# Head scores from two fp32r parts in four row bands instead of three bf16 parts in two, with the expert weights loaded later

## The chip, the cores and the metric

The kernel runs on 1 core of a Trainium2 chip. The metric is the device time of one execution in microseconds (us). A core has TensorE (PE; its weight loads are shown as PEld), VectorE (DVE), ScalarE (ACT), GpSimd (POOL) and SyncE (SP, which here only issues DMAs), each with its own instruction stream; they meet at semaphores.

## The reference, cut to what matters

A layer of attention and a mixture of experts, in fp32, over 32 batches of 256 tokens with 128 features:

```python
qkv = x @ W_qkv.T + b_qkv            # 16 heads, head size 8
att = einsum('bthd,bshd->bhts', q, k) / sqrt(8)
att_v = einsum('bhts,bshd->bthd', softmax(att), v)
x = layernorm(x + att_v @ W_out.T + b_out)
# 8 experts of 128x128, two chosen per token, and a shared one
h = silu(routed @ w1[e].T) * (routed @ w3[e].T);  out = h @ w2[e].T
x = layernorm(x + moe(x))
```

The routing picks the two best experts of each token, so x must be exact enough that no choice flips. This is why scores are built from several parts of lower precision and not from one.

## The kernel before, in words

**Two stages.** The first is attention over 32 batches, the second the experts over 16 groups of 512 tokens. The stages share SBUF: buffers of the second (`places`) lie on `q_stack` and `k_stack`.

**The scores.** The product of q and k over a head has a contraction of only 8. q and k are each split into three bf16 parts on POOL (L428 to L455: casts, differences, remainders `rk`, `rq`), and six pairs of parts (`QPART`, `KPART`) are stacked, so that one matmul with 48 rows gives the exact score. The parts go by DMA to DRAM (L336, L341) and come back stacked (L304): `q_stack` and `k_stack` hold 128 partitions in two halves of 64, even heads in one and odd heads in the other. The scores are computed twice. `row_maxima_scores` (L651) has queries on the output partitions, and DVE reduces 512 columns to negative row maxima (L937). The maxima, as two bf16 parts (POOL L406, L408), are transposed (L784), copied to `max_rows` by DVE (L978) and put by two DMAs (L310) in two more rows of `q_stack`. `shifted_scores` (L638, 50 rows) has keys on the output partitions and includes the maxima; ACT takes the exponential (L515). `values` (L666) multiplies by v in fp32, four heads at a time in column strips of 32. Each of the two kinds of scores has three PSUM banks, used in turn.

**The slots.** The attention is software-pipelined over slots s = -4 to 34. In slot s: SP loads x of batch s+5, q and k of batch s+4 are projected (`t.proj`: L735, L752), batch s+3 is stacked and its v projected (`t.stack`: L748), s+2 has its row maxima (`t.maxi`), s+1 has them transposed and stacked (`t.neg`), s has its exponentials (`t.soft`), s-1 is normalised and transposed (`t.tail`: L768, L806, DVE L971, L987), s-2 goes through output projection and layer norm (`t.norm`: L728, L949 to L959, POOL L435, L444, L800), s-3 through the gate (`t.gated`: L775). Each engine has a fixed order written out in its `slot` function. On TensorE it is eight pairs of heads, p = 0 to 7: 4 shifted-score matmuls and 4 maxima matmuls in turn, then one block of other work: output and K projection after p = 0, values after p = 1, 3, 5 and 7, V and Q projection after p = 2, transposes, gate and maxima after p = 4, transposes back after p = 6. DVE does a reduction per head, with the sum of the residual after head 1, its statistics after 2 and 4, and reciprocal, `max_rows`, `logits` and `att_tok` after head 9.

**The start.** DVE clears `k_stack` and `v_aug` for all four ring places. ACT makes kf and qf of batch 0 and then issues all constants (`load_constants`, L499 and L503): small ones, `w1T`, `w3T`, `w2T` (576 KB each) and 16 DMAs for the v bias. Near slot 0, ACT rounds w1 and w3 to fp32r (L584), and POOL makes the remainders (L461).

**The experts.** 16 groups, each 9 experts: `up` is 2 x 3 fp32r matmuls (L673 to L675), `down` one fp32 matmul (L829), with DVE (L1001, L1011), ACT (L603, L616) and POOL (L476) between; L835 closes the group before.

## Time and profile before

| | us |
|---|---|
| median of 3 runs | 806.11 (803.26 to 808.59) |
| the profiled execution | 806.83 |
| its span, first to last instruction | 804.8 |
| PE busy | 757.6 (94%) |
| DVE busy | 639.9 (80%) |
| ACT busy | 521.4 (65%) |
| POOL busy | 480.6 (60%) |

Busy time is the union of an engine's recorded instructions. Records of one engine can overlap (a matmul's record is longer than the distance to the next), so that an engine whose work is paced by another can still look full. The profile's slices show the two stages: in the first DVE is at nine tenths or more in most slices, in the second at six or seven; PE is at nine tenths in both after the first slices.

### The profile page before, as it was taken

What the parts mean: (1) busy time and instruction counts of PE and PEld (TensorE: products, weight loads), DVE (VectorE), ACT (ScalarE), POOL (GpSimd) and SP (SyncE); (2) the same over time, 40 slices, a digit from 0 to 9 for tenths busy, and PEclk for the clock granted to TensorE, in tenths of its full rate; (3) what the DMA queues carried; (4) which work ended last, traced back from release to release, by engine and by line L of the source; (5) the groups of instructions that cost most, each with busy time, mean ns of one, the idle gap of its engine ahead of it and who ended that gap; (6) DMA issues with size and microseconds to landing.
All of it is one profiled execution on the core that took longest, in us unless ns stands there. A gap on an engine that the chain in (4) does not pass through costs nothing.

```text
span 804.8 us, 18923 instructions
## 1 busy us (share of the span) xinstructions
PE 757.6 (94%) x6148; PEld 460.7 (57%) x6148; DVE 639.9 (80%) x1382; ACT 521.4 (65%) x1047; POOL 480.6 (60%) x653
## 2 busy tenths in 40 slices
PE   1699999999999999999998699999999999999996
PEld 0234555555555555555554466666666666666663
DVE  5578999999999999999997286666666666666765
ACT  1138888888888888888888265555555555555542
POOL 3446767667667677676633345555666565656654
PEclk9999999999999999999999789999999999999998
DMA  5653656656565566566520442455644444444541
GB/s 162 166 128 114 175 160 169 170 157 155 165 165 158 169 169 161 160 166 164 149 76 22 131 116 75 131 132 131 130 129 123 118 126 116 128 119 117 133 120 52
DMA packets 201534, 108.79 MB, mean 135 GB/s; under 512 B 10480, under 2 KB 201072, under 8 KB 201456
## 3 DMA queue, kind: packets, MB, share of 16 engines
q1 hardware_dynamic: 200048, 105.88, 49.5%
q10 hardware_dynamic: 1408, 1.91, 0.9%
q8 instruction: 44, 0.72, 0.4%
q14 instruction: 34, 0.28, 0.1%
HBM read 73.41 MB, written 33.82 MB: 133 GB/s over the span
## 4 chain that ended last, share of the span: by engine, by line
PE 87%; issue 3%; DVE 3%; POOL 3%; DMA 2%; ACT 1%; SPq 1%; POOLq 0%; DVEq 0%; ACTq 0%
PE bank L666 15%; PE bank L829 14%; PE bank L638 10%; PE bank L673 8%; PE bank L675 8%; PE bank L674 8%; PE bank L651 7%; PE bank L748 3%; PE bank L728 2%; PE bank L768 2%; PE bank L735 2%; PE bank L752 2%; PE bank L800 2%; PE bank L775 1%; DVE negmax L937 1%
## 5 line engine op out<-in xcount | busy, mean ns | idle before, releaser
L937 DVE TENSOR_REDUCE negmax<-bank 128x2 f32<-128x512 f32 x512 | 320.1, 679 | 25.3 <-PE bank L651 22.7
L515 ACT ACTIVATE probs<-bank 128x512 f32<-128x512 f32 x512 | 291.7, 605 | 61.0 <-PE bank L638 57.2
L651 PE MATMUL bank<-k_stack,q_stack 48*128 48x256 bf16 x1024 | 163.7, 283 | 9.4 <-DMA k_stack<-k_parts_dram 5.3
L673 PE MATMUL bank<-x_hi,hi_w 128*128 128x512 f32 x288 | 166.5, 578 | 1.3 <-DVE q_stack L1011 0.9
L616 ACT ACTIVATE q_stack<-k_stack 128x512 f32<-128x512 f32 x128 | 80.7, 631 | 122.7 <-DVE k_stack L1001 121.2
L638 PE MATMUL bank<-q_stack,k_stack 50*128 50x256 bf16 x1024 | 156.8, 275 | 2.9 <-ACT probs L515 2.5
L1001 DVE TENSOR_TENSOR k_stack<-bank,probs 128x512 f32<-128x512 f32 x128 | 88.2, 689 | 75.5 <-PE bank L675 69.6
L666 PE MATMUL bank<-probs,v_aug 128*32 128x256 f32 x2048 | 137.9, 387 | 0.4 <-ACT attT L526 0.4
L638 PEld LDWEIGHTS bank<-q_stack,k_stack 50*128 50x128 bf16 x1024 | 75.4, 95 | 86.7 <-ACT probs L515 44.5
L675 PE MATMUL bank<-x_lo,hi_w 128*128 128x512 f32 x288 | 115.3, 400 | 0.0
L674 PE MATMUL bank<-x_hi,lo_w 128*128 128x512 f32 x288 | 115.3, 400 | 0.0
L603 ACT ACTIVATE probs<-probs 128x512 f32<-128x512 f32 x128 | 79.3, 620 | 22.7 <-DMA probs<-route_dram 22.0
L476 POOL TENSOR_TENSOR k_stack<-k_stack,probs 128x512 f32<-128x512 f32 x48 | 61.9, 1290 | 52.8 <-DVE k_stack L1011 47.6
L651 PEld LDWEIGHTS bank<-k_stack,q_stack 48*128 48x128 bf16 x1024 | 71.8, 96 | 27.7 <-DVE negmax L937 11.7
L666 PEld LDWEIGHTS bank<-probs,v_aug 128*32 128x32 f32 x2048 | 53.8, 109 | 49.7 <-issue 15.0
L829 PE MATMUL bank<-k_stack,w_sb 128*128 128x512 f32 x160 | 81.5, 592 | 0.0
L673 PEld LDWEIGHTS bank<-x_hi,hi_w 128*128 128x128 f32 x288 | 55.2, 192 | 39.7 <-issue 28.8
L476 POOL TENSOR_TENSOR k_stack<-q_stack,probs 128x512 f32<-128x512 f32 x32 | 41.1, 1283 | 60.1 <-DVE q_stack L1011 51.2
L476 POOL TENSOR_TENSOR place<-k_stack,probs 128x512 f32<-128x512 f32 x48 | 62.1, 1294 | 24.4 <-PE bank L829 23.5
L674 PEld LDWEIGHTS bank<-x_hi,lo_w 128*128 128x128 f32 x288 | 55.6, 193 | 36.1 <-issue 29.1
L1011 DVE TENSOR_TENSOR k_stack<-bank,q_stack 128x512 f32<-128x512 f32 x96 | 65.5, 682 | 4.3 <-POOL k_stack L476 3.6
L675 PEld LDWEIGHTS bank<-x_lo,hi_w 128*128 128x128 f32 x288 | 55.1, 191 | 13.5
(101 smaller groups left out, 1061.4 us busy)
## 6 DMA issues: line engine op xcount, KB each, us to landing
probs<-route_dram SPq DMA_DIRECT2D x128, 256.0 KB, 5.9
q_stack<-q_parts_dram SPq DMA_DIRECT2D x64, 192.0 KB, 3.3
k_stack<-k_parts_dram SPq DMA_DIRECT2D x64, 192.0 KB, 4.1
k_parts_dram<-k_parts SPq DMA_DIRECT2D x32, 192.0 KB, 2.1
q_parts_dram<-q_parts SPq DMA_DIRECT2D x32, 192.0 KB, 2.1
xT_sb<-xT SPq DMA_DIRECT2D x32, 128.0 KB, 2.2
k_parts_dram<-k_parts SPq DMA_DIRECT2D x32, 128.0 KB, 2.0
q_parts_dram<-q_parts SPq DMA_DIRECT2D x32, 128.0 KB, 2.0
```

Of the source, the lines that this page charges most:

```text
L476: pool.tensor_tensor(hid_s[n % DEPTH], hid[n % DEPTH], weight2_b[n - 1], ALU.mult).then_inc(hids_set, 1)
L515: nc.scalar.activation(probs[h][:], score_ps[EXP_BANK[h]][:].rearrange("p (j t) -> p j t", j=NT), ACT.Exp).then_inc(exp_done, 1)
L616: nc.scalar.activation(act[n % DEPTH], gated[n % DEPTH] if n else up1_ps[0][:], ACT.Silu).then_inc(act_set, 1)
L638: mm = pe.matmul(score_ps[EXP_BANK[h]][:, j * T:(j + 1) * T], k_stack[b.ring][first:last, h // 2, j * P:(j + 1) * P], q_stack[b.ring][firs ...
L651: mm = pe.matmul(max_ps[MAX_BANK[h]][:, i * T:(i + 1) * T], q_stack[b.ring][first:last, h // 2, i * P:(i + 1) * P], k_stack[b.ring][first: ...
L666: mm = pe.matmul(av_ps[32 * hh:32 * hh + 32, half * T:(half + 1) * T], v_aug[b.ring][:, 2 * j + half, u, hh, :], probs[4 * quad + hh][:, j ...
L673: pe.matmul(ps[:], w_hi[m][:, n, :], hi[:], start=start, stop=False)
L674: pe.matmul(ps[:], w_lo[m][:, n, :], hi[:], start=False, stop=False)
L675: return pe.matmul(ps[:], w_hi[m][:, n, :], lo[:], start=False, stop=stop)
L829: pe.matmul(down_ps[r][:], w2_sb[:, n, :], (hid_s if n else hid)[n % DEPTH], start=(n == 0), stop=(n == NE - 1)).then_inc(down_mm, 1)
L937: nc.vector.tensor_reduce(negmax[b.ring % 2][:, :, column], max_ps[MAX_BANK[h]][:].rearrange("p (i s) -> p i s", i=NT), AX_X, ALU.max, neg ...
L1001: nc.vector.tensor_tensor(gated[n % DEPTH], up1_ps[n % DEPTH][:], weight_b[e], ALU.mult).then_inc(gated_set, 1)
```

## The change: what it does

- q and k are split into two fp32r parts instead of three bf16 parts; three pairs of parts make 24 rows a head (26 with the maxima) instead of 48 (50). POOL issues 4 split operations a batch instead of 8.
- The stacks hold four bands of 32 partitions, one head of four in each, as 4-byte elements: `[128, 4 heads, 256]` instead of `[128, 8, 256]` in bf16, the same bytes. The score matmuls are fp32r. Shifted scores use band h % 4, maxima take head h ^ 2, so that the four matmuls of one step of a pair lie in four different bands. The loops over n (which half of the 256) and h change places, so that both heads of a pair are worked on together.
- SP issues 2 DMAs each for the parts of k and q (3 before), 8 for the stacks (4 before), 4 for the maxima (2 before). `max_rows` is fp32, 8 of its partitions to a DMA.
- For batch 0, q is projected into `av_ps` without waiting for kf, and split by DVE between the clearing of ring places 1 and 2. ACT waits for the clearing of the place that it writes, not for all four.
- The small constants are issued at the end of the slot that projects batch 1; w1, w3 and w2 one by one in slots 2, 3 and 4; their split is done in six pieces in slots 4 to 9. The v bias takes 2 DMAs to DRAM and one back instead of 16.
- In the expert stage, `places` lie elsewhere, the load of `x1_sb` is issued after the weights of the group, and a group's result is written one group later in SP's order.

```diff
-PARTS = 3
-QPART = (0, 0, 0, 1, 1, 2)
-KPART = (0, 1, 2, 0, 1, 0)
-TWO_ONES = float(np.array([0x3F803F80], np.uint32).view(np.float32)[0])
+PARTS = 2
+QPART = (0, 0, 1)
+KPART = (0, 1, 0)
 HALF = 64
+FOUR, BAND = 4, 32
...
+        q_stack = [sb(f"q_stack{r}", [P, QUADS, T]) for r in range(RING)]
+        k_stack = [sb(f"k_stack{r}", [P, QUADS, T]) for r in range(RING)]
...
+        qf, kf = (sb(n, [P, T]) for n in ("qf", "kf"))
+        q_parts, k_parts = ([sb(f"{n}{r}", [P, PARTS, T], F32R) for r in range(2)] for n in ("q_parts", "k_parts"))
+        max_two = [sb(f"max_two{r}", [P, NT, FOUR, 2, QUADS], BF16) for r in range(2)]
+        max_rows = sb("max_rows", [2 * H, T])
...
+        def steps(b, more):
+            return more if b.c == 0 else b.count(4, more - 2)
+        def expert_slot(m):
+            return 2 + m
+        def split_slot(m, n):
+            return 4 + m * (NE // 3) + n // 3
+        def q_place(b):
+            return av_ps[:, 0:T] if b.c == 0 else right
...
-                        for u in range(2):
-                            sp.dma_start(stack[b.ring][HALF * u:HALF * u + ROWS, :, :],
-                                         dram[b.ring].rearrange("(g u) d c t -> u (d c) g t", u=2)[u]).then_inc(stack_in[b.ring], 16)
+                        for u in range(FOUR):
+                            sp.dma_start(stack[b.ring][BAND * u:BAND * u + ROWS, :, :],
+                                         dram[b.ring].rearrange("(g u) d c t -> u (d c) g t", u=FOUR)[u]).then_inc(stack_in[b.ring], 16)
                 b = t.neg
                 if b.live:
                     sp.wait_ge(max_rows_set, b.count(1, 1))
-                    for u in range(2):
-                        sp.dma_start(q_stack[b.ring][HALF * u + ROWS:HALF * u + ROWS + 2, :, :],
-                                     max_rows[H * u:H * u + H, :]).then_inc(max_in[b.ring], 16)
+                    for u in range(FOUR):
+                        sp.dma_start(q_stack[b.ring][BAND * u + ROWS:BAND * u + ROWS + 2, :, :],
+                                     max_rows[2 * QUADS * u:2 * QUADS * (u + 1), :]).then_inc(max_in[b.ring], 16)
...
-                    sp.wait_ge(split_step, b.count(8, 4))
-                    for part in range(PARTS):
-                        first, count = QPART.index(part), QPART.count(part)
-                        assert KPART[first:first + count] == tuple(range(count))
-                        sp.dma_start(k_parts_dram[b.ring, :, :, first:first + count].rearrange("h d c t -> (h d) c t"),
-                                     k_parts[b.ring % 2][:, 0:count, :]).then_inc(parts_out, 16)
-                    sp.wait_ge(split_step, b.count(8, 8))
-                    for part in range(PARTS):
-                        first, count = QPART.index(part), QPART.count(part)
-                        sp.dma_start(q_parts_dram[b.ring, :, :, first:first + count].rearrange("h d c t -> (h d) c t"),
-                                     q_parts[b.ring % 2][:, part:part + 1, :].to_broadcast([P, count, T])).then_inc(parts_out, 16)
+                    sp.wait_ge(split_step, steps(b, 2))
+                    k_place, k_from = k_parts_dram[b.ring].rearrange("h d c t -> (h d) c t"), k_parts[b.ring % 2][:].bitcast(F32)
+                    sp.dma_start(k_place[:, 0:2], k_from).then_inc(parts_out, 16)
+                    sp.dma_start(k_place[:, 2:3], k_from[:, 0:1]).then_inc(parts_out, 16)
+                    if b.c == 0:
+                        sp.wait_ge(q_split_set, 2)
+                    else:
+                        sp.wait_ge(split_step, steps(b, 4))
+                    q_place, q_from = q_parts_dram[b.ring].rearrange("h d c t -> (h d) c t"), q_parts[b.ring % 2][:].bitcast(F32)
+                    sp.dma_start(q_place[:, 0:2], q_from[:, 0:1].to_broadcast([P, 2, T])).then_inc(parts_out, 16)
+                    sp.dma_start(q_place[:, 2:3], q_from[:, 1:2]).then_inc(parts_out, 16)
...
-                    if e == 4:
+                    if e == E - 1:
                         if past(g, 2):
                             sp.wait_ge(res2_set, g - 1)
                         sp.dma_start(x1_sb[r][:], x1_dram[bass.ds(g * GT, GT), :, :].rearrange("i p c -> p i c")).then_inc(x1_in[r], 16)
-                    if e == 3 and past(g, 2):
-                        write_out(g - 1)
+                    if e == 3 and past(g, 3):
+                        write_out(g - 2)
                 if isinstance(g, int) and g == 1:
                     route_to_dram(slice(CHUNKS - 1, CHUNKS), 2)
                     sp.wait_ge(route_out[1], 16)
 
             groups(sp, group)
+            write_out(GROUPS - 2)
...
-                    pool.wait_ge(split_step, p.count(8, 1))
-                    pool.tensor_tensor(rk[:], kf[:], k_split[:, 0, :], ALU.subtract).then_inc(split_step, 1)
...
+                if p.live and p.c:
                     pool.wait_ge(qk_f, p.count(2, 2))
-                    pool.tensor_tensor(k_split[:, 2, :], rk[:], k_split[:, 1, :], ALU.subtract).then_inc(split_step, 1)
                     pool.tensor_copy(q_split[:, 0, :], qf[:]).then_inc(split_step, 1)
-                    pool.wait_ge(split_step, p.count(8, 5))
-                    pool.tensor_tensor(rq[:], qf[:], q_split[:, 0, :], ALU.subtract).then_inc(split_step, 1)
+                    pool.wait_ge(split_step, steps(p, 3))
                     pool.tensor_tensor(q_split[:, 1, :], qf[:], q_split[:, 0, :], ALU.subtract).then_inc(split_step, 1)
-                    pool.wait_ge(split_step, p.count(8, 7))
-                    pool.tensor_tensor(q_split[:, 2, :], rq[:], q_split[:, 1, :], ALU.subtract).then_inc(split_step, 1)
-                    if p.c == RING and not p.looped:
-                        for m in range(2):
-                            pool.wait_ge(w_hi_set, m + 1)
-                            pool.tensor_tensor(w_lo[m][:], w_stage[m], w_hi[m][:], ALU.subtract).then_inc(w_lo_set, 1)
+                for m in range(2):
+                    for n in range(0, NE, 3):
+                        if t.soft.c == split_slot(m, n):
+                            pool.wait_ge(w_hi_set, m * (NE // 3) + n // 3 + 1)
+                            pool.tensor_tensor(w_lo[m][:, n:n + 3, :], w_stage[m][:, n:n + 3, :], w_hi[m][:, n:n + 3, :],
+                                               ALU.subtract).then_inc(w_lo_set, 1)
...
-                                 (gate_sb, gateT), (ebias_sb, ebias.to_broadcast([P, E])), (rank_sb, rank.to_broadcast([P, E])),
-                                 (w_stage[0], w1T), (w_stage[1], w3T), (w2_sb, w2T)):
+                                 (gate_sb, gateT), (ebias_sb, ebias.to_broadcast([P, E])), (rank_sb, rank.to_broadcast([P, E]))):
                     act_e.dma_start(dst[:], src).then_inc(c_in, 16)
-                for head in range(H):
-                    half, u, hh = head // 8, head // 4 % 2, head % 4
-                    row = half * 64 + hh * 2 * D + u * D
-                    act_e.dma_start(bv_sb[row:row + D, :], bv[0, 0:1, head * D:head * D + D].rearrange("o d -> d o")).then_inc(bv_in, 16)
+                for half in range(2):
+                    act_e.dma_start(bv_dram[HALF * half:HALF * half + HALF].rearrange("(g u d) o -> g u (d o)", g=4, u=2),
+                                    bv[0, 0:1, HALF * half:HALF * half + HALF].rearrange("o (u g d) -> (o g) u d", u=2, g=4)).then_inc(bv_out, 16)
+            def load_expert(m):
+                dst, src = ((w_stage[0], w1T), (w_stage[1], w3T), (w2_sb, w2T))[m]
+                act_e.dma_start(dst[:], src).then_inc(expert_in[m], 16)
...
-                            load_constants()
-                    if b.live and h == 12 and b.c == RING and not b.looped:
-                        act_e.wait_ge(c_in, 16 * 8)
+                        if b.c == 1:
+                            act_e.wait_ge(q_split_set, 2)
+                        elif b.later(1):
+                            act_e.wait_ge(split_step, steps(Batch(b.i, b.c - 1, B), 4))
+                        nc.scalar.activation(qf[:], q_place(b), ACT.Identity, bias=bqs[:, 0:1], scale=SCALE).then_inc(qk_f, 1)
+                    if b.live and h == 12:
                         for m in range(2):
-                            nc.scalar.activation(w_hi[m][:], w_stage[m], ACT.Copy).then_inc(w_hi_set, 1)
+                            for n in range(0, NE, 3):
+                                if t.soft.c == split_slot(m, n):
+                                    act_e.wait_ge(expert_in[m], 16)
+                                    nc.scalar.activation(w_hi[m][:, n:n + 3, :], w_stage[m][:, n:n + 3, :], ACT.Copy).then_inc(w_hi_set, 1)
+                        for m in range(3):
+                            if t.soft.c == expert_slot(m):
+                                load_expert(m)
+                if t.proj.c == 1:
+                    load_constants()
+                if t.proj.c == 2:
+                    act_e.wait_ge(bv_out, 16 * 2)
+                    act_e.dma_start(bv_sb[:], bv_dram).then_inc(bv_in, 16)
...
-                    pe.wait_ge(max_in[b.ring], b.lap(32, 32))
-                    if b.c == 0 and not b.looped:
-                        pe.wait_ge(c_in, 16 * 8)
+                    pe.wait_ge(max_in[b.ring], b.lap(64, 64))
                 if j == 0 and (b.later(1) or h >= EXP_BACK[h]):
                     pe.wait_ge(exp_done, b.count(H, h + 1 - EXP_BACK[h]))
-                first, last = HALF * (h % 2), HALF * (h % 2) + ROWS + 2
-                mm = pe.matmul(score_ps[EXP_BANK[h]][:, j * T:(j + 1) * T], k_stack[b.ring][first:last, h // 2, j * P:(j + 1) * P],
-                               q_stack[b.ring][first:last, h // 2, :], start=True, stop=True)
+                first, last = BAND * (h % FOUR), BAND * (h % FOUR) + ROWS + 2
+                mm = pe.matmul(score_ps[EXP_BANK[h]][:, j * T:(j + 1) * T],
+                               k_stack[b.ring][first:last, h // FOUR, j * P:(j + 1) * P].bitcast(F32R),
+                               q_stack[b.ring][first:last, h // FOUR, :].bitcast(F32R), start=True, stop=True)
                 if j == NT - 1:
                     mm.then_inc(score_mm, 1)
 
             def row_maxima_scores(b, h, i):
 
                 if i == 0 and h == 0:
-                    pe.wait_ge(stack_in[b.ring], b.lap(64, 64))
+                    pe.wait_ge(stack_in[b.ring], b.lap(128, 128))
                 if i == 0 and (b.later(1) or h >= MAX_BACK[h]):
                     pe.wait_ge(max_red, b.count(H, h + 1 - MAX_BACK[h]))
-                other = 1 - h % 2
-                first, last = HALF * other, HALF * other + ROWS
-                mm = pe.matmul(max_ps[MAX_BANK[h]][:, i * T:(i + 1) * T], q_stack[b.ring][first:last, h // 2, i * P:(i + 1) * P],
-                               k_stack[b.ring][first:last, h // 2, :], start=True, stop=True)
+                m = h ^ 2
+                first, last = BAND * (m % FOUR), BAND * (m % FOUR) + ROWS
+                mm = pe.matmul(max_ps[MAX_BANK[h]][:, i * T:(i + 1) * T],
+                               q_stack[b.ring][first:last, m // FOUR, i * P:(i + 1) * P].bitcast(F32R),
+                               k_stack[b.ring][first:last, m // FOUR, :].bitcast(F32R), start=True, stop=True)
...
-                    for h in (2 * p, 2 * p + 1):
-                        for n in range(NT):
+                    for n in range(NT):
+                        for h in (2 * p, 2 * p + 1):
...
+                        if t.proj.live and t.proj.c:
...
+                        pe.matmul(q_place(b), wq_sb[:], xT_sb[b.ring][:], start=True, stop=True).then_inc(q_mm, 1)
...
-            for r in range(RING):
-                flat = k_stack[r][:].rearrange("p h t -> p (h t)").bitcast(F32)
-                for u in range(2):
-                    dve.memset(flat[HALF * u + 32:HALF * u + HALF, :], TWO_ONES).then_inc(k_ones, 1)
+            def clear(r):
+                dve.memset(k_stack[r][:], 1.0).then_inc(k_ones, 1)
                 dve.memset(v_aug[r][:], 0.0).then_inc(v_clear, 1)
                 dve.wait_ge(v_clear, 2 * r + 1)
                 for u in range(2):
                     ins = dve.memset(v_aug[r][:, :, u, :, 2 * D + u:2 * D + u + 1], 1.0)
                 ins.then_inc(v_clear, 1)
+            clear(0)
+            clear(1)
+            q_split = q_parts[0]
+            dve.wait_ge(qk_f, 2)
+            nc.vector.tensor_copy(q_split[:, 0, :], qf[:]).then_inc(q_split_set, 1)
+            dve.wait_ge(q_split_set, 1)
+            nc.vector.tensor_tensor(q_split[:, 1, :], qf[:], q_split[:, 0, :], ALU.subtract).then_inc(q_split_set, 1)
+            clear(2)
+            clear(3)
...
-                        column = PAIRS * (1 - h % 2) + h // 2
+                        m = h ^ 2
+                        column = QUADS * (m % FOUR) + m // FOUR
```

## Rows read from the trace of the kernel before

**Rows 1.** By stretch: length; busy of PE, PEld, DVE, ACT, POOL; clock, DMA share, GB/s:
```profile
202.17:214.65 12.48, 12.48 (x156) 7.11 (x154) 12.19 (x27) 10.57 (x24) 8.56 (x16) 1.00 0.61 161
...
393.30:405.20 11.90, 11.66 (x151) 6.68 (x151) 11.64 (x27) 9.89 (x22) 7.46 (x14) 1.00 0.45 120
...
500.00:520.00 20.00, 20.00 (x76) 13.53 (x74) 13.17 (x26) 10.35 (x19) 12.55 (x10) 1.00 0.47 125
```

**Rows 2.** Timeline of TensorE: K projection of two slots, 24 slots apart:
```profile
92.03 0.60 PE L735 MATMUL bank<-xT_sb,wk_sb 128*128 128x256 f32 x2
...
387.41 0.38 PE L735 MATMUL bank<-xT_sb,wk_sb 128*128 128x256 f32 x1
```

**Rows 3.** Timeline of TensorE: the transposes of two neighbouring slots without projections:
```profile
405.15 0.44 PE L768 MATMUL bank<-used_first,attT 128*128 128x128 f32 x2
...
417.10 0.55 PE L768 MATMUL bank<-used_first,attT 128*128 128x128 f32 x3
```

**Rows 4.** Timeline of TensorE: one pair's scores and the values behind it:
```profile
203.25 0.28 PE L638 MATMUL bank<-q_stack,k_stack 50*128 50x256 bf16 x1
...
203.60 0.27 PE L638 MATMUL bank<-q_stack,k_stack 50*128 50x256 bf16 x1
203.79 1.07 PE L666 MATMUL bank<-probs,v_aug 128*32 128x256 f32 x16
```

**Rows 5.** Timeline of the weight loads, the same pair and the V projection:
```profile
203.25 0.09 PEld L638 LDWEIGHTS bank<-q_stack,k_stack 50*128 50x128 bf16 x1 [0.33 <-ACT probs L515]
203.25 0.09 PEld L651 LDWEIGHTS bank<-k_stack,q_stack 48*128 48x128 bf16 x1
...
203.79 0.59 PEld L666 LDWEIGHTS bank<-probs,v_aug 128*32 128x32 f32 x16 [0.21 <-issue]
...
205.34 0.52 PEld L748 LDWEIGHTS bank<-wv_sb,xT_sb 128*128 128x128 f32 x4 [0.21 <-issue]
```

**Rows 6.** Timeline of VectorE in one slot:
```profile
203.36 0.42 DVE L949 TENSOR_TENSOR res<-bank,x_bo 128x256 f32<-128x256 f32 x1
...
206.28 0.43 DVE L959 TENSOR_SCALAR var_eps<-mv 128x2 f32<-128x2 f32 x1
206.63 3.08 DVE L937 TENSOR_REDUCE negmax<-bank 128x2 f32<-128x512 f32 x5
209.86 0.36 DVE L971 RECIPROCAL recip_sum<-bank 128x32 f32<-128x32 f32 x1
...
210.86 4.40 DVE L937 TENSOR_REDUCE negmax<-bank 128x2 f32<-128x512 f32 x7
```

**Rows 7.** The line L959 alone, in the two slots without projections:
```profile
L959 DVE TENSOR_SCALAR var_eps<-mv x2: 169/169/169, 403.2 to 415.1; 128x2 f32<-128x2 f32 x2
```

**Rows 8.** Timelines of DVE, SP and PE: from the maxima's copy to the next slot:
```profile
222.62 0.21 DVE L978 COPY max_rows<-bank 32x256 bf16<-32x256 bf16 x1
...
222.86 1.26 SPq L310 DMA_DIRECT2D q_stack<-max_rows  x2
...
226.41 0.28 PE L638 MATMUL bank<-q_stack,k_stack 50*128 50x256 bf16 x1
```

**Rows 9.** The chain of waits at the start (start, us, what):
```profile
13.18 8.54 DMA q_parts_dram<-q_parts
...
23.12 4.29 DMA k_stack<-k_parts_dram
...
27.55 0.61 PE bank L651 x4
...
48.70 0.82 SPq L310
49.57 1.89 DMA q_stack<-max_rows
```

**Rows 10.** Timeline of ACT near slot 0:
```profile
64.41 2.21 ACT L584 ACTIVATE hi_w<-x1T 128x1152 fp32r<-128x1152 f32 x2
```

More of the change, by code:

```diff
@@ L133, in attention_moe_layer @@
         w_in, xT_in, x_in = sem("w_in"), [sem(f"xT_in{r}") for r in range(RING)], [sem(f"x_in{r}") for r in range(RING)]
-        c_in = sem("c_in")
+        c_in, bv_out, expert_in = sem("c_in"), sem("bv_out"), [sem(f"expert_in{m}") for m in range(3)]
+        q_split_set = sem("q_split_set")
         k_ones, v_clear, consts_set = sem("k_ones"), sem("v_clear"), sem("consts_set")
@@ L196, in attention_moe_layer @@
         LAG, HID_LAG = 4, 1
-        places = [stack[:].rearrange("p h t -> p (h t)").bitcast(F32)[:, n * G:(n + 1) * G]
-                  for stack in q_stack[:2] + k_stack[:2] + q_stack[2:] + k_stack[2:] for n in range(PAIRS * T // 2 // G)]
-        places += [sb(f"place{n}", [P, G])[:] for n in range(8)]
+        places = [parts[:].rearrange("p c t -> p (c t)").bitcast(F32) for parts in q_parts + k_parts]
+        places += [sb(f"place{n}", [P, G])[:] for n in range(10)]
+        places += [v[:].rearrange("p a u g c -> p (a u g c)")[:, n * G:(n + 1) * G] for v in v_aug for n in range(2)]
+        places += [attT[:].rearrange("p a t -> p (a t)")]
+        assert PARTS * T == G
         def take(count):
@@ L551, in slot @@
                             act_e.wait_ge(av_mm, b.count(4, 4 * (1 - RING)))
-                        elif not b.later(1):
-                            act_e.wait_ge(v_clear, 2 * RING)
+                        else:
+                            act_e.wait_ge(v_clear, 2 * (b.c + 1))
                         for u in range(2):
@@ L751, in slot @@
                     if b.live and p == PE_VQ:
-                        pe.matmul(right, wq_sb[:], xT_sb[b.ring][:], start=True, stop=True).then_inc(q_mm, 1)
+                        pe.matmul(q_place(b), wq_sb[:], xT_sb[b.ring][:], start=True, stop=True).then_inc(q_mm, 1)
                     if p == PE_TOK:
```

51 lines of the change are left out of this document (22 added, 29 removed).

## The prediction

> **What bounds the kernel now.** I read the busy time by stretch first. A slot of attention takes 12.3 to 12.5 us; in the one shown TensorE is busy for all of its 12.48 us and DVE for 12.19 [rows 1]. The distance of two K projections, 24 slots apart, gives the pitch: (387.41 - 92.03) / 24 = 12.31 us [rows 2]. In the expert stage TensorE is busy for 20.00 of 20.00 us, and DVE for only 13.17 [rows 1]. So TensorE sets the pace of both stages, but in attention DVE stands just behind it. How close, the two slots without projections tell: there TensorE has less to do and idles, and the pitch falls only to 417.10 - 405.15 = 11.95 us [rows 3]. That is DVE's own pace. I check it with DVE's timeline [rows 6]. Five reductions whose record is 0.68 us each span 3.08, so one follows another after (3.08 - 0.68) / 4 = 0.60 us, and 16 take 9.6. From the residual's sum at 203.36 to the reductions at 206.63 there are 3.27 us with three reductions in them, so 1.47 for sum, statistics and variance; reciprocal to `att_tok` take 210.86 - 209.86 = 1.00. The sum is 12.07 us. The slots without projections have a shorter L959: 0.17 us [rows 7] instead of 0.43 [rows 6]; in them POOL has no splitting to do.
>
> **The score matmuls.** A pair of heads takes 203.79 - 203.25 = 0.54 us before the next block starts [rows 4]: the last matmul starts 0.35 after the first, and 0.19 more go by until the next block. Eight matmuls go in pairs, one in each half of the array, four steps of 0.115. The change makes it two steps of four. Against it stands the weight load: bf16 loads have records of 0.09 us, the four fp32 loads of 128 columns span 0.52 with a mean of 0.19, so they follow each other after (0.52 - 0.19) / 3 = 0.11 us [rows 5]. No row shows an fp32r load in a band of 32 rows. I take 0.11, from that row. If the loads of four bands run side by side, a pair costs 0.11 for the first loads, 0.11 for one step and 0.19 until the next block: 0.41, 0.13 less, times 8 pairs = 1.05 us a slot, and TensorE needs 12.3 - 1.05 = 11.25. They do run side by side as far as rows show: the loads of the two halves both start at 203.25, and 16 fp32 loads in four strips of columns take 0.59 us together with records of 0.11 [rows 5]. The bounds are 0.30 a pair (nothing for the loads: 2 x 0.115 less than now, minus 0.01) and 1.07 (eight loads of 0.11 in turn, then 0.19).
>
> The Trainium skill (TensorE: Matmul & The Clock Gate, "Weight-path perf modes") says that the fast weight load is on only for 128 weights and types other than FP32. The records of 0.09 against 0.19 us agree. It speaks against this change, which takes the fast load away from 64 loads a slot. TensorEngine Tiling (Array Packing) of the same skill, "Key Properties", says that different tiles can load weights and multiply in parallel; by that the loss is paid once per pair, otherwise four times per step. No row shows four bands.
>
> **What a slot becomes.** With TensorE at 11.25, DVE is the bound. POOL issues four subtractions of 256 columns fewer, among them the one beside L959; this gives DVE up to 0.26 back: 12.07 - 0.26 = 11.8. Two things work against it. First, a pair now needs both its banks free before its first matmul, so TensorE can be less far ahead: pairs followed by values take 0.41 + 1.0 = 1.41 us on TensorE against 1.20 for two reductions, and DVE's surplus of work at the start of a slot and at the transposes makes up for all but some 0.16. That gives 11.96. Second, the maxima need four DMAs instead of two. SP issues two in 1.26 us, so 0.63 each; the copy ends at 222.83 and the next slot's scores start at 226.41, 3.58 later [rows 8]. At the start of the kernel, second issue to landing took 1.89 [rows 9], so landing is now some 2.5 after the copy and becomes 2.5 + 1.26 = 3.76 at 0.63 an issue, 3.4 at 0.45. DVE at its own pace wants the scores 3.5 after the copy. I take 0.1 to 0.15 for it: 12.1 us a slot. Gain: 0.2 x 24 = 4.8 us; with POOL's gift not given and the DMAs at 0.63, 12.3 or more and nothing or a loss; with neither drag 11.8 and 12. SP's other issues: stacks 4 more, parts 2 fewer; SP has some 7.4 us of issues in 12.3 now, and the stack issues end about 2 us before the maxima, so those 4 x 0.47 = 1.9 are just hidden; without that cover they delay the maxima's DMAs one for one. The two slots before the layer norms run (68 to 92) were paced by TensorE and gain about 0.4 each: 0.8. Exponentials on ACT (10.57 of 12.48 busy) stay hidden. The drain at the end of attention gains 0.3.
>
> **The start.** On the chain, the parts of q of batch 0 take 8.54 us to land after 13.18, while 1.7 MB of constants are on the way; the stack follows with 4.29 from 23.12, and the first maxima start at 27.55 [rows 9]. After the change: kf at 6.7 as now, two POOL operations (0.4 + 0.7), k's DMAs at 7.9. q's projection no longer waits for kf, ACT finishes qf near 7.5, DVE has cleared two places by 6 and splits q by 8.2. SP issues four DMAs by 9.9; without the constants they land after about 2.1 (as the maxima's 1.89): 11.7. Then 8 stack DMAs instead of 4: 8 x 0.47 = 3.8, the last lands 3 to 4 after its issue: 18.5. So 27.55 - 18.5 = 9.0 us earlier; from both sides: 6 if the eight DMAs queue behind each other, 10.5 if the last lands in 2. In slot 0 TensorE waits for the maxima's DMAs openly, so the two added issues cost 2 x 0.63 = 1.2. The constants now issue after batch 1's projections, in a gap of ACT: nothing, with 3 us of cover.
>
> **The expert weights.** ACT's rounding took 2.21 us in one piece in front of the exponentials of slot 0 [rows 10] and was on the chain: gain 2.0. Six pieces of 0.4 in six slots hide under ACT's idle 1.7 us; uncovered, 2.4. Three loads of 576 KB in slots 2 to 4 add about a third to a slot's DMA traffic, whose share is 0.61 [rows 1]: 0, at most 1 us each if they delay the maxima.
>
> **The expert stage** is paced by TensorE, whose work is unchanged. The other order of SP's DMAs moves loads that nobody waits for there: 0; its price without cover would be under 1 us a group.
>
> **Sum.** 9.0 - 1.2 + 2.0 + 0.8 + 4.8 + 0.3 = 15.7 us. Against the profiled execution (806.83; span 804.8 and 2.0 around it; 0.7 over the median of the runs shown): 791.
>
> **Rivals.**
> (a) The maxima's DMAs set the slot. Their place is the first pair of each slot. They decide once landing is later than 3.5 us after the copy; at 4.1 (stack issues in their way, or longer landing of 1 KB rows) a slot is 12.5: 0.2 x 24 = 4.8 lost instead of 4.8 gained: 800.5. For it: 3.76 by the rows is already late. Against: an issue with half the rows may be shorter.
> (b) Slower than before: the bands' loads or matmuls take turns. The place is each pair; it decides once a step of four takes more than (0.54 - 0.19) / 2 = 0.175 us. With eight loads of 0.11 a pair costs 1.07, 0.53 more, 4.2 a slot: 16.5; over some 28 slots + 118, less 10.9 of start: 914. Weaker form: the matmuls need two passes as fp32 does, steps of 0.22 and a pair of 0.62: 12.95 a slot, + 16 - 11 = 812. Against both: the equal start times of the halves' loads [rows 5].
> (c) The start gains little, because the eight stack DMAs queue and batch 1 is late: 3 instead of 9: 797.
> (d) The change doesn't relieve TensorE at all (a pair stays at 0.54): slots of 12.3, start as forecast: 796.
>
> **How the numbers follow.** A measurement of this kernel can tell about 1% (8 us) from no change. Forecast case: 0.60, own range 784 to 797. (a) 0.12, (b) 0.09 (0.05 for turns, 0.04 for two passes), (c) 0.10, (d) 0.09. The predicted time is 791. The range of 782 to 803 leaves out (b) and the far ends of the others, 0.15 to 0.2 together. Faster by over 1% (under 798): 0.59 from the forecast case, 0.03 from (a), 0.07 from (c), 0.08 from (d): 0.77. Slower by over 1% (over 814): the first form of (b) and most of what lies above 812 of the second: 0.08. Within 1%: the rest, 0.15.
>
> **What the profile after would show.** First maxima near 18.5 us. The four score matmuls of a step within 0.02 us of each other, steps 0.11 apart, the next block 0.41 after the pair's first. TensorE busy under 95% of a slot and DVE without gaps; L959 at 0.17. Pitch 12.1. If the first pair of each slot waits for the maxima's DMAs, (a) is right; if weight loads of the bands start 0.11 apart, (b). A group of experts stays at its pace. I am wrong if DVE shows gaps of over 0.5 us a slot behind TensorE, or if the start moves by less than 6.

## Result and profile after

| | before | after |
|---|---|---|
| median, us | 805.94 (803.26 to 808.59) | 824.16 (824.00 to 824.83) |
| profiled execution, its span | 806.83, 804.8 | 824.21, 822.4 |

After over before is 1.0229, 95% interval 1.0202 to 1.0257: slower by 18 us, where the forecast was 15 us faster. Some executions of one and the same kernel are over 1.5% longer than its fastest, at a lower granted clock; the ranges below hold them, the ratios leave them out.

The stretches come first: four slots, cut at their K projections, then a late one. Columns as in [rows 1]; PEclk is the share of TensorE's full clock that was granted, 1.00 or, at half clock, 0.50, averaged over the stretch.

```profile
core 0: us, PE busy (x) PEld busy (x) DVE busy (x) ACT busy (x) POOL busy (x), PEclk, DMA share, GB/s
75.87:91.09 15.22, 12.69 (x153) 7.75 (x151) 12.21 (x27) 11.02 (x25) 6.01 (x11) 0.94 0.68 215
91.09:109.18 18.09, 15.84 (x156) 9.14 (x155) 11.69 (x26) 10.41 (x24) 6.02 (x11) 0.77 0.41 127
109.18:126.49 17.31, 15.11 (x156) 8.91 (x155) 12.06 (x27) 11.28 (x26) 7.00 (x12) 0.80 0.50 153
126.49:140.39 13.90, 13.67 (x157) 7.91 (x155) 12.10 (x27) 10.84 (x26) 6.93 (x12) 0.88 0.36 109
202.00:214.50 12.50, 12.16 (x154) 7.54 (x154) 11.64 (x27) 10.29 (x24) 5.85 (x11) 1.00 0.52 161
```

See two things. The late slot is 12.5 us, not 12.1, at full clock, and neither TensorE nor DVE fills it. And the slots in which the expert weights arrive take up to 18.09 at a granted clock of 0.77 to 0.94.

The chain of waits in a late slot says why it is 12.5 (start, us, what):

```profile
210.47 0.36 DVE max_rows L1017
...
210.85 0.62 SPq L331
...
211.51 0.62 SPq L331
...
212.17 0.61 SPq L331
...
212.83 1.88 DMA q_stack<-max_rows
...
214.75 0.38 PE bank L662
```

Four issues in a row (the fourth is inside the 1.88, which counts from its start to the landing): 214.71 - 210.83 = 3.88 us from copy to landing, as the next slot's scores begin. The first issue starts 0.02 us after the copy, so the eight stack DMAs are not in the way here. In one late slot they are (298.95, 0.76 after the copy), and it takes 13.23 instead of 12.49. In [rows 8] the scores began 3.58 after the copy, after work on TensorE. The waits from 160 to 390 us (total, times, longest) show it in each of the 18 slots counted, and DVE's gap of 0.58 a slot is over the 0.5 that the prediction named as a sign of being wrong:

```profile
PEld bank L662 <- DMA q_stack<-max_rows: 12.8, 18, 1.4
DVE negmax L976 <- PE bank L676: 10.5, 18, 1.3
```

The page's chain of the end has SP's queue and DMAs in it now:

```profile
PE 49%; DVE 22%; SPq 11%; DMA 10%; issue 6%; POOL 1%; ACT 1%; POOLq 0%; DVEq 0%; ACTq 0%
```

In slot 3 the same chain reads differently in one line, and the DMA view names what was beside it (KB, median us to landing):

```profile
104.14 3.91 DMA q_stack<-max_rows
```

```profile
x1T<-w3T ACTq DMA_DIRECT2D x1, 576.0 KB, 3.9
```

The load was issued at 103.63, 1.5 us after the first of the maxima's DMAs and before the fourth. That fourth one lands after 3.91 us instead of 1.88. TensorE idles up to 2.8 us for it, and half clock follows.

What was forecast well: the first maxima at 18.83 (forecast 18.5, before 27.55), and a pair of heads. These are TensorE's timeline and the weight loads of a pair, to set beside [rows 4] and [rows 5]:

```profile
203.89 0.38 PE L662 MATMUL bank<-q_stack,k_stack 26*128 26x256 f32 x1
203.89 0.38 PE L676 MATMUL bank<-k_stack,q_stack 24*128 24x256 f32 x1
...
204.11 0.28 PE L662 MATMUL bank<-q_stack,k_stack 26*128 26x256 f32 x1
...
204.33 0.85 PE L692 MATMUL bank<-probs,v_aug 128*32 128x256 f32 x12
```

```profile
203.89 0.18 PEld L662 LDWEIGHTS bank<-q_stack,k_stack 26*128 26x128 f32 x1 [0.33 <-issue]
203.89 0.18 PEld L676 LDWEIGHTS bank<-k_stack,q_stack 24*128 24x128 f32 x1
203.90 0.18 PEld L662 LDWEIGHTS bank<-q_stack,k_stack 26*128 26x128 f32 x1
203.90 0.18 PEld L676 LDWEIGHTS bank<-k_stack,q_stack 24*128 24x128 f32 x1
204.00 0.18 PEld L662 LDWEIGHTS bank<-q_stack,k_stack 26*128 26x128 f32 x1
```

Four loads start within 0.01 us, the next four 0.11 later. The Trainium skill (TensorEngine Tiling (Array Packing), "Key Properties") says that different tiles can load weights and multiply in parallel. For the loads the trace agrees; for the matmuls see the exchanged loops below. The pair's block is 204.33 - 203.89 = 0.44 us, but two steps of 0.22, not 0.11 + 0.11 + 0.19.

**Where the 17.6 us of the spans lie**, by the K projections of both traces (slots counted from the first with exponentials, a slot from its K projection to the next; positive is lost; the forecast's 0.8 for 68 to 92 us lies half in slot 1 and half in slot 2):

| stretch | before | after | forecast | difference |
|---|---|---|---|---|
| to the first slot's K projection | 28.14 | 19.55 | -9.0 | -8.6 |
| slots -2 to 1 | 51.96 | 56.32 | -1.2 | +4.4 |
| slots 2 to 5 | 48.88 | 64.52 | -1.0 | +15.6 |
| to the last K projection | 258.48 | 263.49 | -4.2 | +5.0 |
| the end | 417.3 | 418.5 | -0.3 | +1.2 |

### The profile page after: what moved, and what is told of

It is laid out like the page before. It is cut to its first block, busy times and chain, and to the rows that moved or that the text cites. A ratio compares the mean times of both kernels' runs of the same rounds, so it can differ in the third digit from the quotient of the medians.

```text
span 822.4 us, 18922 instructions
## 1 busy us (share of the span) xinstructions
PE 766.7 (93%) x6148; PEld 488.4 (59%) x6148; DVE 635.1 (77%) x1380; ACT 518.7 (63%) x1051; POOL 399.6 (49%) x527
## 4 chain that ended last, share of the span: by engine, by line
PE 49%; DVE 22%; SPq 11%; DMA 10%; issue 6%; POOL 1%; ACT 1%; POOLq 0%; DVEq 0%; ACTq 0%
DVE negmax L976 16%; PE bank L858 14%; PE bank L699 8%; PE bank L701 8%; PE bank L700 8%; SPq L331 7%; DMA q_stack<-max_rows 7%; PE bank L662 4%; PE bank L692 2%; DMA q_parts_dram<-q_parts 2%; SPq L325 2%; PE bank L676 2%; DVE max_rows L1017 1%; DVE stats L991 1%; PE bank L764 1%
## 5 line engine op out<-in xcount | busy, mean ns | idle before, releaser
L491 POOL TENSOR_TENSOR v_aug<-place,probs 128x512 f32<-128x512 f32 x128 | 164.5, 1290 | 136.9 <-DVE place L1050 94.5
L642 ACT ACTIVATE place<-place 128x512 f32<-128x512 f32 x128 | 80.8, 631 | 147.9 <-DVE place L1040 146.4
L676 PE MATMUL bank<-k_stack,q_stack 24*128 24x256 f32 x1024 | 156.7, 351 | 15.1 <-DMA k_stack<-k_parts_dram 7.4
L662 PE MATMUL bank<-q_stack,k_stack 26*128 26x256 f32 x1024 | 149.4, 344 | 17.7 <-DMA q_stack<-max_rows 14.7
L662 PEld LDWEIGHTS bank<-q_stack,k_stack 26*128 26x128 f32 x1024 | 89.8, 189 | 106.5 <-ACT probs L532 62.1
L1040 DVE TENSOR_TENSOR place<-bank,probs 128x512 f32<-128x512 f32 x128 | 88.2, 689 | 76.4 <-PE bank L701 76.1
L858 PE MATMUL bank<-v_aug,w_sb 128*128 128x512 f32 x256 | 130.3, 592 | 0.0
L1050 DVE TENSOR_TENSOR place<-bank,place 128x512 f32<-128x512 f32 x144 | 98.5, 684 | 21.2 <-PE bank L858 14.2
L676 PEld LDWEIGHTS bank<-k_stack,q_stack 24*128 24x128 f32 x1024 | 95.4, 196 | 28.8 <-DVE negmax L976 17.7
L858 PEld LDWEIGHTS bank<-v_aug,w_sb 128*128 128x128 f32 x256 | 48.1, 189 | 13.5 <-POOL v_aug L491 1.6
```

The source lines that it names most:

```text
L491: pool.tensor_tensor(hid_s[n % DEPTH], hid[n % DEPTH], weight2_b[n - 1], ALU.mult).then_inc(hids_set, 1)
L662: mm = pe.matmul(score_ps[EXP_BANK[h]][:, j * T:(j + 1) * T], k_stack[b.ring][first:last, h // FOUR, j * P:(j + 1) * P].bitcast(F32R), q_s ...
L676: mm = pe.matmul(max_ps[MAX_BANK[h]][:, i * T:(i + 1) * T], q_stack[b.ring][first:last, m // FOUR, i * P:(i + 1) * P].bitcast(F32R), k_sta ...
L858: pe.matmul(down_ps[r][:], w2_sb[:, n, :], (hid_s if n else hid)[n % DEPTH], start=(n == 0), stop=(n == NE - 1)).then_inc(down_mm, 1)
L1040: nc.vector.tensor_tensor(gated[n % DEPTH], up1_ps[n % DEPTH][:], weight_b[e], ALU.mult).then_inc(gated_set, 1)
L1050: nc.vector.tensor_tensor(hid[n % DEPTH], up3_ps[n % DEPTH][:], act[n % DEPTH], ALU.mult).then_inc(hid_set, 1)
```

## Experiments

Two causes were set against each other: the four maxima's DMAs, in each slot, and the expert loads beside them, in slots 2 to 4, with the clock that follows. Each kernel is timed against the kernel before on its chip (804.0 to 806.2 us).

**The expert loads away from the maxima's DMAs**, in the changed kernel:

```
-  (after head 12)      for m in range(3): if t.soft.c == expert_slot(m): load_expert(m)
+  if b.live and h == 3:
+                       for m in range(3): if t.soft.c == expert_slot(m): load_expert(m)
```

> The changed kernel, but w1, w3 and w2 are issued after head 3 of slots 2, 3 and 4 instead of after head 12. Theory: the three loads of 576 KB are issued 1.4 us after the first of the maxima's DMAs and delay their landing from 1.9 to 3.9 us; TensorE then waits 2.3 to 2.8 us and its granted clock falls to half, so slots 2 to 5 take 15.2, 18.1, 17.3 and 13.9 us. Moved away from the maxima, these slots take 12.5 to 12.7 and the time falls from 824 to about 810. Rival 1: what slows these slots is ACT's rounding pieces and POOL's remainders (slots 4 to 9), which stay: no change, 822 to 824. Rival 2: the thin fp32r matmuls themselves let the clock fall in the early slots: the half-clock stretches stay, 818 or more.

Measured 814.18 us (812.47 to 815.89), 10.0 less than the changed kernel, where about 14 were expected. Two of the slots with loads, at full clock again:

```profile
91.20:103.70 12.50, 12.24 (x154) 7.54 (x154) 11.82 (x27) 10.48 (x24) 5.96 (x12) 1.00 0.71 209
103.70:116.10 12.40, 12.25 (x154) 7.55 (x154) 11.82 (x27) 10.47 (x24) 6.88 (x12) 1.00 0.74 209
```

Slots 2 to 5 take 14.5 us less together, 4.8 a load. Slots 0 and 1, whose code is the same, took 3.9 more here: TensorE ran at half its speed for longer (a K projection at 64.72 still takes 1.22 us, where 0.60 is full speed). The same bytes nine heads of sixteen earlier cost nothing that shows here. ACT's rounding and the fp32r matmuls, the two rivals, stayed as they were, so neither had slowed slots 2 to 5. The ratio is still 1.0105 (1.0032 to 1.0177): the rest of the loss is elsewhere.

**Four maxima's DMAs in the kernel before**, one for each row of each half:

```
-  sp.dma_start(q_stack[b.ring][HALF*u+ROWS : HALF*u+ROWS+2], max_rows[H*u : H*u+H]).then_inc(max_in[b.ring], 16)
+  for m in range(2):
+      sp.dma_start(q_stack[b.ring][HALF*u+ROWS+m : HALF*u+ROWS+m+1], max_rows[H*u+PAIRS*m : H*u+PAIRS*(m+1)])...
```

> The kernel before (bf16, two halves) with four DMAs for the maxima instead of two, one per row of each half. Theory: the landing moves from some 2.5 to 3.8 us after the copy, past the 3.58 that the next slot's scores stand away, so the pitch grows from 12.31 to about 12.5 and the time from 806 to 809 to 813. Rival (the pitch of 12.49 comes from the bands or from fp32r, not from the number of DMAs): pitch stays at 12.31 and the time at 806.

Measured 820.57 (819.33 to 821.22), ratio 1.0179 (1.0125 to 1.0233): the two added issues alone cost 14 us, more than the 3 to 7 expected, and a slot is 12.70 us instead of 12.30. Why it is 0.40 here and 0.28 with bands is not shown. Its waits have the changed kernel's line:

```profile
PEld bank L639 <- DMA q_stack<-max_rows: 14.2, 18, 1.5
```

**Two maxima's DMAs in the changed kernel**: the rows in the order part, band, quad, so that one strided DMA fills four bands:

```
-  for u in range(FOUR):
-      sp.dma_start(q_stack[b.ring][BAND*u+ROWS : BAND*u+ROWS+2], max_rows[2*QUADS*u : 2*QUADS*(u+1)])...
+  for m in range(2):
+      sp.dma_start(q_stack[b.ring][ROWS+m::BAND], max_rows[H*m : H*(m+1)])...
```

> The changed kernel with two DMAs for the maxima, as the kernel before has: the rows of max_two and max_rows are ordered so that one DMA writes row 24 and one row 25 of all four bands. Expert loads stay after head 12 of slots 2 to 4. Theory: four issues of 0.65 us put the landing 3.9 us after the copy and set the pitch of 12.49; two put it at 2.6, and DVE becomes the bound: pitch 11.95 to 12.1, some 10 us over the stage, and the loads' delay of 2 us is partly covered: 804 to 812. Rival (a pair needs both its banks free, so DVE is starved between pairs): pitch 12.3 to 12.4 and only the slots 2 to 5 gain: 812 to 820.

Measured 805.55 (804.97 to 828.08), ratio 1.0018 (0.998 to 1.0056). The late slot is 12.21, between the theory's 11.95 to 12.1 and the rival's 12.3 to 12.4. Slots 3 and 4 still took 16.09 and 15.64, by one late landing. The loads of slots 2 and 4 were issued 0.8 and 0.9 us behind the second and last of the maxima's DMAs, and TensorE waits for none. In slot 3 the parts for the stack landed late (after 5.09 us) and one stack issue took 1.39 us instead of 0.38, so SP reached the maxima a microsecond late. The load, issued at 93.75, was now ahead of the second of their DMAs, which landed after 5.05:

```profile
89.36 1.39 SPq L325
...
93.31 0.54 SPq L331
...
93.89 5.05 DMA q_stack<-max_rows
```

TensorE waits 2.96 us and then has half clock for some 10. What a single DMA for all the maxima would bring was not measured.

**Both edits:**

> Both edits: two DMAs for the maxima, expert loads after head 3 of slots 2 to 4. Theory: 814 less some 10 us: 800 to 806, pitch 11.95 to 12.1. Rival (pairs starve DVE): pitch 12.3 to 12.4, 809 to 813.

Measured 800.45 (796.59 to 805.24), ratio 0.9961 (0.9934 to 0.9988). The time is the expected one, the slot of 12.21 again neither theory's nor rival's. Together the two causes make up the loss. The same stretches in the four kernels with bands:

| stretch, us | changed kernel | loads moved | two DMAs | both |
|---|---|---|---|---|
| slots -2 to 1 | 56.32 | 60.24 | 52.79 | 52.77 |
| slots 2 to 5 | 64.52 | 49.99 | 56.10 | 48.99 |
| to the last K projection | 263.49 | 263.06 | 256.75 | 256.77 |
| the end | 418.5 | 421.1 | 417.7 | 417.1 |

In slots 2 to 5 the loads cost 14.5 us beside four DMAs and 7.1 beside two. The two added DMAs cost 3.5 us in the first slots, 1.0 in slots 2 to 5 without the loads in their way (8.4 with them), and 6.3 to 6.7 behind.

What bounds the slot then? The stretch, and a piece of the chain:

```profile
232.00:244.20 12.20, 12.13 (x155) 7.51 (x154) 11.88 (x27) 10.53 (x24) 6.04 (x11) 1.00 0.59 188
```

```profile
239.45 0.61 DVE negmax L977
240.06 0.04 issue
240.10 0.38 PE bank L677
```

No wait for the maxima's DMAs is left from 160 to 390 us. DVE works 11.88 of 12.20. TensorE's eight pairs, each from its first matmul to the next block, take 0.44, 0.45, 0.51, 0.55, 0.44, 0.88, 0.56 and 0.44: 4.27 us, where 8 x 0.44 would be 3.52. So TensorE alone would need 12.21 - 0.75 = 11.46, and is held for a bank by DVE; then DVE waits 0.3 for it. The prediction has a first drag for this, of 0.16. But DVE stands idle for nearly as long in halves, too (12.04 of 12.30 us in the kernel with late loads below, 11.64 of 11.90 in [rows 1]), so most of the 0.3 is not the bands'.

**Is it the order within a pair?** Both edits, and the loops over heads and blocks of queries exchanged, so that a head's bank is needed only when its turn comes:

```
-  for n in range(NT):
-      for h in (2 * p, 2 * p + 1):
+  for h in (2 * p, 2 * p + 1):
+      for n in range(NT):
```

> The kernel with both edits, and the loops over the heads of a pair and over n as the kernel before has them: a head's two halves follow each other, so that only two bands work at a time, but the first head's bank is full earlier and the second head needs its bank later. If pairs starve DVE (the rival), this is faster than e3 or equal, in the half-clock slots at the start above all. If the four bands at once are what relieves TensorE, a pair takes 0.11 to 0.25 us longer, TensorE is again at 12.2 and the time is that of e3 plus 3 to 8 us.

The slot stayed at 12.20. The time, 808.81 (795.99 to 821.03), can't be used for a few us: the profiled run had half clock for 30.7 us in attention's last slots. The ratio, 0.9931 (0.9896 to 0.9966), can't be told from that of both edits. One pair a slot still takes 0.88 (232.15 to 233.03), so waiting by heads instead of by pairs brings nothing; how much of the 0.3 comes from the pair's two banks and how much from DVE's own gaps isn't settled.

The other branch, 0.11 to 0.25 more a pair, has not come either: a pair takes 0.44 us in this order too (235.22 to 235.66), although by the edit a head's four matmuls use two bands only. That four bands work at once is thus not what brought the pair from 0.54 to 0.44. What did is not shown.

**The loads in thirds**: nine pieces of 192 KB after head 12 of slots 2 to 10:

```
-  act_e.dma_start(dst[:], src)                        # one each in slots 2, 3, 4
+  act_e.dma_start(dst[:, n:n+3], src[:, n:n+3])       # nine, in slots 2 to 10
```

> The changed kernel with the expert weights loaded in nine pieces of 192 KB after head 12 of slots 2 to 10 (same place beside the maxima's DMAs, same bytes, a third at a time; rounding in slots 6 to 11). Theory: each piece delays the landing by a third of 2.05 us, TensorE waits about 1 us more per slot and the clock stays: nine slots at about 13.2, none at half clock: 808 to 818 against 824. Rival (the place beside the maxima costs 2 us whatever the size, or fp32r lets the clock fall): nine slots of 14.5 or more, 830 to 845.

Measured 817.82 (816.90 to 818.74): 6.3 less than the changed kernel, 3.6 more than with the loads moved. The slots are 12.7 to 14.3 us; the landings beside a piece 2.17 to 3.37 instead of 1.88. The slot behind the longest of them has a clock of 0.88, the other eight 1.00. A smaller transfer delays less, but there are nine of them. Place beats size.

**The same load late, where TensorE has long been at full clock**: the kernel with the loads moved, and w2 loaded twice more, again between the third and the fourth of the maxima's DMAs, in slots 14 and 20:

```
+  if t.soft.c in (14, 20):
+      act_e.wait_ge(expert_in[2], 16 if t.soft.c == 14 else 32)
+      load_expert(2)
```

> The changed kernel with its expert loads off the maxima (814 us), plus the 576 KB of w2 loaded again right behind the maxima's DMAs in slots 14 and 20, where TensorE has long been at 1.00. The loads change nothing that is computed. Theory (a 576 KB load beside the four maxima DMAs makes them land about 2 us later, TensorE waits for it, and the clock falls after that wait): landing 3.9 instead of 1.9 us, TensorE waits 2 to 3 us, a stretch at half clock follows, each of the two slots with its successor 3 to 6 us longer: 820 to 826 us. Rival 1 (only the late landing counts, the clock stays 1.00): +1.5 to 2 each, 817 to 818 us. Rival 2 (what was slow in slots 2 to 4 was the first slots, not the loads): 814 us.

Measured 824.08 (822.64 to 825.52): 9.9 more than with the loads moved, for two loads. Chain, TensorE's timeline, then the stretches around the first one:

```profile
237.00 3.75 DMA q_stack<-max_rows
...
254.28 1.88 DMA q_stack<-max_rows
```

```profile
240.79 0.38 PE L666 MATMUL bank<-q_stack,k_stack 26*128 26x256 f32 x1 [2.08 <-DMA q_stack<-max_rows]
```

```profile
227.49:242.48 14.99, 12.84 (x156) 8.07 (x155) 12.38 (x28) 11.07 (x25) 6.02 (x11) 0.95 0.68 216
242.48:257.29 14.81, 14.57 (x156) 8.68 (x156) 11.67 (x26) 10.31 (x23) 6.01 (x11) 0.82 0.33 97
257.29:269.79 12.50, 12.26 (x157) 7.57 (x156) 11.91 (x27) 10.55 (x25) 6.02 (x11) 1.00 0.52 161
```

Maxima land 1.9 late, TensorE waits, and in this and in the other case half clock is granted for 6.8 us behind the wait. Between K projections two slots take 14.99 + 14.81 instead of 2 x 12.49: 4.8 us; the other pair 14.46 + 15.42: 4.9. In that pair the two prices stand apart: 14.46 at a clock of 1.00, then 15.42 at 0.78. So about 2 us of a load's price is the wait and 3 the clock. That the loads met the kernel in its first slots is not what made them dear. The Trainium skill (DMA: Bandwidth & Descriptors, "Issuing engines are not separate DMA queues") says that issuing from several engines saves only the sequencer's time. The trace agrees: ACT's load delays SP's 8 KB.

**Only the late loads, without bands**: the kernel before with the change's late constants, its few DMAs for the v bias and its late expert loads (at the fourth head), rounded in six pieces:

```
-  (first batch)  load_constants()      # with w1, w3, w2; rounding in one piece in slot 0
+  if t.proj.c == 1: load_constants()   # without them
+  if b.live and h == 3: ... load_expert(m)       # slots 2, 3, 4
```

> The kernel before, with its bf16 halves and its two maxima DMAs, and only the late loads of the change: constants at the first projected group, the expert weights in slots 2 to 4 at the fourth head (not beside the maxima's DMAs), their rounding in six pieces in slots 4 to 9. Theory (the start was gained by the late loads, not by the bands): first maxima from 27.6 us to about 19, the slot of 15.43 us with the rounding goes back to about 12.3, the steady slot stays 12.30, so 806 - 8.5 to 11 = about 796 us. Rival (the start was gained by the bands, or the early slots run at half clock whenever they start earlier, as in the bands' 13.4, 13.6): the early slots lengthen by 1 to 2 us each and the time is 800 to 804.

Measured 798.53 (797.88 to 799.25), ratio 0.9919 (0.9890 to 0.9947). Its first groups on TensorE:

```profile
20.69 0.61 PE L667 MATMUL bank<-k_stack,q_stack 48*128 48x256 bf16 x4 [8.32 <-DMA k_stack<-k_parts_dram]
21.23 1.22 PE L754 MATMUL bank<-xT_sb,wk_sb 128*128 128x256 f32 x2
```

and of the changed kernel:

```profile
18.83 0.79 PE L676 MATMUL bank<-k_stack,q_stack 24*128 24x256 f32 x4 [7.42 <-DMA k_stack<-k_parts_dram]
19.55 1.22 PE L764 MATMUL bank<-xT_sb,wk_sb 128*128 128x256 f32 x2
```

Of the 8.7 us of start, 6.9 come from the late constants and 1.9 from the rest of the change: the bands, and q of batch 0 on a way of its own, which weren't tried apart. But the two K matmuls take 1.22 us here and 0.60 later, so TensorE runs at half its speed (the clock's column says 1.00 there, and in the changed kernel until 60 us), and a pair's maxima then cost the bands 0.72 us against 0.54. Slots -2 to 0 are 11.99, 12.47 and 12.67 here, 13.43, 13.58 and 13.50 with bands and both edits: the bands lose 3.4 us again (eight pairs at 0.18 more are 1.44 a slot, which is what slot -2 shows). The rounding in pieces takes the slot of 15.43 to 12.67: 2.8. The load at the fourth head is not quite free here: slot 2 takes 13.04 (12.77 when the kernel ran again) instead of 11.98. Slots 3 and 4 stay at 12.30.

**Bands against halves once more, on one chip**, the kernels of "both edits" and of the late loads unchanged:

> The bands with two maxima DMAs and the expert loads off the maxima once more, now on one chip with the halves that have the same late loads (next kernel). Theory (the bands' steady slot is 12.21 against 12.30 us, but their slots -2 to 0 are about 1 us longer each): 24 slots x 0.09 = 2.2 us gained, 2 to 3 lost at the start, so the two agree within 2 us, both about 797 to 799 us. Rival (the bands still bring what the change wanted of them): 3 us or more faster than the halves.

> The halves of the kernel before with the late loads: 798.5 us measured; again 797 to 800 us, steady slot 12.30. Within 2 us of the bands by the theory, 3 us or more slower than they by the rival.

Bands 803.13 (795.80 to 817.39, 12 runs), ratio 0.9953 (0.9931 to 0.9975); halves 797.64 (795.69 to 798.60), ratio 0.9902 (0.9885 to 0.9920). The halves came as expected. The bands did not: they are 5.5 us slower by the medians and 0.5% by the ratios, neither the theory's 2 us nor the rival's gain. Up to the last K projection the theory holds, which both profiled runs reach at the same time, 378.16 and 378.15. The rest is behind it. In the profile of the bands attention's last slots ran at half clock:

```profile
406.00:437.00 31.00, 30.17 (x219) 16.95 (x219) 17.05 (x37) 16.79 (x33) 6.61 (x11) 0.50 0.08 24
```

It begins behind a wait of TensorE for DVE, 1.07 us at 406.14. The same kernel's other profile has the same wait at 406.01 and keeps 1.00, and the halves have 0.99 at 405.75. So the wait alone doesn't decide it, and why the bands' kernels meet this more often stays open. The two kernels also differ in the end of attention and in the order of SP in the expert stage; that was not tried apart. The best version measured is the kernel before with the late loads alone: 1.0% under before, 3.2% under the changed kernel.

## Why the prediction was wrong

- **The expert loads: the step that failed most in the sum.** "0, at most 1 us each if they delay the maxima" was 4.8 us each: 14.5 in slots 2 to 5 by the run that moves them, 4.8 and 4.9 for one by the late loads. I counted bytes against a slot's traffic. The load is issued among the DMAs with the least slack in the slot, and delays the last of them by 2 us; behind the wait comes half clock, 6.8 us of it in each of the two late cases, a second price that had no term. In slots 2 to 5, 16.6 of the 33 us of error lie.
- **The maxima's DMAs: mechanism right, size wrong.** Forecast 0.1 to 0.15 a slot, measured 12.49 - 12.21 = 0.28 with bands and 0.40 with halves: 7 to 10 us over 24 slots, and 3.5 in the first slots. Copy to landing was forecast as 3.76 from the rows, measured 3.88. By the prediction's own threshold of 3.5 that is 0.26 a slot; it took about half of this, between the 0.26 and the nothing of an issue of 0.45, which no row had (measured 0.62). By whole runs this step is the dearer one: two DMAs give 19.2 us of span back, the moved loads 8.3 (12.2 but for slots 0 and 1), since it also decides how many loads hit. Rival (a) gave 12.5 a slot, which is what came, at a chance of 0.12; its 3.76 was already over its own threshold. But its time, 800.5, is as far off, since the loads had no price in it either.
- **DVE's pace and the drag.** Its own pace was forecast as 11.8; busy is 11.88. L959's gift was right (0.17 us, the line is L998 now). The copy of the maxima takes 0.35 us as a cast to fp32 instead of 0.21: a term that I missed. The drag is 0.3, not 0.16, and 0.26 of it stands in the halves. Without late DMAs a slot is 12.21, not 11.96, so the bands are worth 0.09 a slot, 2.2 us in all, where 4.8 were forecast with the DMAs' price already off. The 0.4 each for slots 1 and 2 are not there: 12.25 and 12.07 with both edits, 12.08 and 11.98 before.
- **The score matmuls: the price right, partly by luck.** 0.44 for 0.41, and the loads start side by side. But the make-up was wrong: two steps of 0.22 instead of 0.11 + 0.11 + 0.19. A step of 0.22 is over the 0.175 at which rival (b) was to decide, and is the one of its weaker form; that the pair is still 0.10 shorter than before contradicts this test, and four bands at once are not the reason, by the exchanged loops.
- **Slots -2 to 1.** Forecast 1.2 gained, measured 4.4 lost: 3.4 for the bands' dearer pairs at half clock, which no term had (slots -2 to 0), 3.5 for the four DMAs, waited for openly (44.62 to 46.51 the landing of 1.89), less 2.8 for the rounding.
- **The start: right**, 8.7 for 9.0. Rival (c) is out; 6.9 of it were never the bands'. Rounding in pieces: 2.8 for 2.0.
- **The end and the expert stage**: 0.3 gain forecast, 1.2 lost. Two profiles of one kernel, the halves with late loads, differ by 2.9 there (418.5 and 415.6), so this says nothing.

## What to carry to other kernels

A small DMA that the next stage waits for is priced from copy to landing against the moment at which its reader can start, not against the engine behind it; two more issues of 0.63 us each cost some 14 us here over 32 slots. Put a large load where no such DMA is about to be issued or in flight: its place in the slot decided between 0 to 1 and 5 us, and smaller pieces did not replace that. And where TensorE has to wait, count what it loses at half clock afterwards beside the wait.

## What the runs showed of the hardware

- An 8 KB transfer that SP issues right behind a 576 KB load on ACT's queue lands after 3.75 to 3.93 us instead of 1.88; a 16 KB one took 5.05 once. Two loads issued 0.8 and 0.9 us behind the last such transfer made TensorE wait for none.
- Behind TensorE's waits of some 2 us the granted clock was half for 6.8 us twice in late slots, behind one of 2.96 for some 10; a slot with such a stretch had 0.75 to 0.95. Behind a wait of 1.07 us it was half for over 30 us in one execution and stayed 1.00 in another of the same kernel.
- In the first 60 us the clock's column shows 1.00 while two K matmuls take 1.22 us, where 0.60 is full speed.
- Eight fp32r matmuls of 24 or 26 rows take 0.44 us, in two steps of 0.22 for 256 columns, at full clock, also with the loops exchanged, when a head's four matmuls use two bands only; at half clock the steps are 0.38 and 0.35. The bf16 pairs in halves of [rows 4] step by 0.115. A pair's maxima alone take 0.72 at half clock, against 0.54 in bf16.
- The copy of 32 x 256 out of PSUM takes DVE 0.35 us as a cast from bf16 to fp32 and 0.22 as a bf16 copy.
